# Turning normalized rows on VectorE and through DRAM instead of on TensorE

## The chip, the core and the metric

The kernel runs on one core of a Trainium2 chip. The time is device microseconds of one execution, the median of three runs. A profile is taken of a further execution; its rows are what this document reads. Engines are named as in the profile: PE is TensorE (PEld its weight loads), DVE VectorE, ACT ScalarE, POOL GpSimd, SP the engine that issues most DMAs; "SPq" is SP's queue.

## The reference

Four batches of 2048 tokens with 256 channels go through four residual steps. LN is a layer norm without learned scale, all in float32:

```
x = x + attention_a(LN(x))     # 16 heads of 16, causal softmax, q k v o projections
x = x + ffn(LN(x))             # sigmoid(W_r xr) * (W_v relu(W_k xk)^2), xr and xk mix x with the row before
x = x + attention_b(LN(x))     # keys: decayed sum, length 1, per-head scale; queries are the next keys;
                               # values: mixed with the next row, length 1, per-head scale
x = x + ffn(LN(x))
```

## The kernel before

**The main loop.** The two attentions of four batches are eight; each is worked in four groups of four heads, which makes NI x NHG = 32 "instances". An instance has NG = 68 groups, in four chunks of queries (qc), whose last slots are 4, 17, 38 and 67. In each slot TensorE computes the scores of the group three ahead (AHEAD = 3, three pairs of PSUM banks) and the probability-value products of its own; ScalarE does the exponentials (L828); GpSimd masks the diagonal groups (L731), which are groups 0 to 4, 13 to 17, 34 to 38 and 63 to 67; VectorE takes a finished chunk out of PSUM with a transpose (`take`, L1493), normalizes it, and in odd instances turns it and hands it to SP, which stores it in `o_chan` (L494) two slots later.

**Side work.** Everything else is a `Job` of one chunk of 512 tokens of one batch, laid into the same slots:
- P: layer norm, turn to channel-major (`xT`), q, k and v projections of attention a (parts u0 to u3, v0, v1), a bound on the scores (n).
- MA: output projection of attention a (o0, o1), layer norm, turn into `xf`, the FFN (k0, k1, r0, r1, f0, f1), a second layer norm (lnb), a second turn into `xT`, keys and values of attention b (bk, bv, vt), their lengths, and the split of keys into three bfloat16 parts.
- MB: output projection of attention b and the second FFN.

Each job has a first slot t0 and a table of offsets (`T_P`, `T_P0`, `T_P1`, `T_M`, `T_B`, `T_END`). MA jobs and most MB jobs start 4 slots before an instance does, so offset 20 is slot 16. Every engine has a program of its own in order of slots (`interleaved`: the main loop's work of a slot first, then the jobs'). No engine counts slots at run time: each works through its own order as fast as its semaphore waits allow, so a wait holds all that stands behind it on that engine.

**Banks.** Six PSUM banks hold scores at any time; side parts use the one of banks 6 and 7 that the current chunk's products don't use. `free_bank` therefore makes a part wait for the take of the chunk before (`s_o`):

```
            def free_bank(part):
                if part.before:
                    pe.wait_ge(s_side[part.bank], part.before)
                if part.seg > 0:
                    pe.wait_ge(s_o, part.seg)
```

**Turns.** A turn is two parts of four TensorE transposes with an identity (`turn`, L884), each copied out of PSUM (`copy_out`, L1204, on VectorE; L771 on ScalarE for batch 0). There are 64: 16 in P jobs, 32 in MA jobs, 16 in MB jobs. In FFN jobs the difference with the row before follows (`buf_a`, L681 on GpSimd and L1329 on VectorE), then four products with mu (L1335), which k0 and r0 wait for.

**Lengths.** In an MA job GpSimd squares keys and values; VectorE reduces both (L1386, L1389), runs one Newton chain over 128 columns (`rsqrt`, L1171 to L1180, L1395 to L1401), gives GpSimd `v_fac` (which it waits for at "vb" to write `v_st`, L709), and scales the keys (L1413).

## Time and profile before

| | |
|---|---|
| median of 3 runs | 3010.7 us (3007.7 to 3011.1) |
| the profiled execution | 3010.8 us, span 3009.1 us |
| mean granted TensorE clock | 0.976 |
| busy: PE, PEld | 2862.4 us, 1302.0 us |
| busy: ACT, DVE, POOL | 2232.7, 1472.8, 817.1 us |
| DMA packets | 229828, 225 MB; SP's queue takes 25.3% of the 16 DMA engines' span |

A busy time is the union of an engine's instructions; matmuls overlap, so a busy TensorE needn't be at its peak. Idle time stands with the instruction that came after it, put down to the semaphore that ended it. In the groups of instructions "out<-in" names tiles, then partitions x elements. Instance n begins where ScalarE does its group 68 n.

### The profile page before, as it was taken

To read this page: it belongs to the slowest core of one execution; us is meant where nothing else is said; L and a number is where in the kernel's file an instruction comes from. 1 tells how busy PE (TensorE), PEld (TensorE's weight loads), DVE (VectorE), ACT (ScalarE), POOL (GpSimd) and SP (SyncE) were. 2 spreads that over 40 slices of the span, in tenths; PEclk is the share of its full clock that TensorE was granted. 3 is DMA by queue.
4 is the path that set the end of the run, shared out by engine and by line. 5 is a ranking of instruction groups with operands and counts; after the bars stand their busy time and mean duration, and the time that the engine had idled before them with its cause. 6 is when DMAs were issued, how large, how long until landed. Compare 5 with 4: busy or idle time off the path is not lost.

```text
span 3009.1 us, 99722 instructions
## 1 busy us (share of the span) xinstructions
PE 2862.4 (95%) x42984; PEld 1302.0 (43%) x42984; DVE 1472.8 (49%) x3579; ACT 2232.7 (74%) x2487; POOL 817.1 (27%) x1246
## 2 busy tenths in 40 slices
PE   6999999999999899998999999999999989999897
PEld 3444444444444344444444444444444434444343
DVE  5322346565556654445344434555665656523544
ACT  2799978787787478784788878778787856788472
POOL 4222223332323222221222222232333322322111
PEclk9999999999999899998999999999999999999898
DMA  5322312222222123222322223222222221222111
GB/s 136 106 83 81 95 53 78 70 73 67 81 71 60 52 67 103 81 76 67 95 81 74 82 89 94 64 78 68 63 75 71 73 66 52 72 72 85 41 62 41
DMA packets 229828, 225.34 MB, mean 75 GB/s; under 512 B 33221, under 2 KB 212933, under 8 KB 229320
## 3 DMA queue, kind: packets, MB, share of 16 engines
q1 hardware_dynamic: 228504, 217.47, 25.3%
q8 instruction: 356, 5.83, 0.8%
q14 instruction: 152, 1.25, 0.1%
q10 hardware_dynamic: 816, 0.79, 0.1%
HBM read 146.80 MB, written 71.32 MB: 72 GB/s over the span
## 4 chain that ended last, share of the span: by engine, by line
PE 72%; DVE 16%; issue 6%; ACT 4%; POOL 1%; SPq 0%; DVEq 0%; DMA 0%; ACTq 0%
PE ps L872 46%; PE ps L1103 23%; ACT probs L828 4%; DVE pmax L1434 3%; PE ps L884 3%; DVE xn L1198 2%; DVE nw_y L1180 1%; DVE nw_u L1178 1%; DVE ln_st L1186 1%; DVE nw_u L1176 1%; DVE x_buf L1315 1%; DVE o_blk L1493 1%; DVE k_blk L1413 1%; DVE nw_v L1389 1%; POOL buf_k L703 0%
## 5 line engine op out<-in xcount | busy, mean ns | idle before, releaser
L828 ACT ACTIVATE probs<-ps 128x1024 f32<-128x1024 f32 x2176 | 2083.1, 1059 | 477.7 <-PE ps L872 474.5
L872 PE MATMUL ps<-q_st,k_st 99*32 99x512 bf16 (+3 forms) x20480 | 1237.4, 349 | 5.0 <-issue 2.4
L1103 PE MATMUL ps<-probs,v_st 128*17 128x512 f32 (+3 forms) x10240 | 1160.7, 532 | 22.4 <-POOL probs L731 13.1
L872 PEld LDWEIGHTS ps<-q_st,k_st 99*32 99x32 bf16 x20480 | 567.0, 96 | 775.7 <-issue 449.6
L731 POOL TENSOR_SCALAR_AFFINE_SELECT probs<-probs 128x256 f32<-128x256 f32 (+1 forms) x896 | 433.4, 501 | 1138.7 <-ACT probs L828 1120.1
L1103 PEld LDWEIGHTS ps<-probs,v_st 128*17 128x17 f32 x10240 | 291.9, 98 | 272.2 <-issue 59.1
L872 PE MATMUL ps<-xT,wT 128*32 128x512 f32 x2048 | 242.6, 594 | 0.0
L1493 DVE STREAM_TRANSPOSE o_blk<-ps 128x512 f32<-128x512 f32 x128 | 91.0, 711 | 269.2 <-PE ps L1103 268.9
L657 POOL TENSOR_TENSOR parts<-rest,parts 128x512 bf16<-128x512 f32 x96 | 120.9, 1260 | 316.7 <-DVE parts L1221 316.7
L1348 DVE SCALAR_TENSOR_TENSOR buf_v<-buf_v,ps 128x512 f32<-128x512 f32 x64 | 44.0, 687 | 272.9 <-PE ps L872 272.9
L1315 DVE TENSOR_TENSOR x_buf<-x_buf,ps 128x512 f32<-128x512 f32 x64 | 43.8, 684 | 217.6 <-PE ps L872 207.2
L872 PE MATMUL ps<-wT,o_in 128*32 128x256 f32 x2048 | 124.3, 380 | 14.5 <-issue 14.5
L872 PE MATMUL ps<-buf_k,wT 128*32 128x512 f32 x1024 | 124.7, 609 | 8.2 <-DVE buf_k L1335 8.0
L872 PEld LDWEIGHTS ps<-xT,wT 128*32 128x32 f32 x2048 | 65.1, 109 | 139.8 <-issue 136.1
L872 PE MATMUL ps<-wT,buf_u 128*32 128x256 f32 x2048 | 121.9, 379 | 1.6 <-issue 1.6
L872 PE MATMUL ps<-wT,buf_a 128*32 128x256 f32 x2048 | 121.6, 379 | 0.6 <-issue 0.5
L884 PE MATMUL ps<-ident,xn 128*128 128x128 f32 x512 | 85.8, 293 | 34.7 <-DVE xn L1198 24.5
L792 ACT ACTIVATE buf_u<-ps 128x512 f32<-128x512 f32 x64 | 38.2, 597 | 99.9 <-PE ps L872 99.9
L884 PEld LDWEIGHTS ps<-ident,xn 128*128 128x128 f32 x512 | 55.8, 145 | 125.1 <-DVE xn L1198 63.1
L1216 DVE TENSOR_TENSOR rest<-ps,parts 128x512 f32<-128x512 f32 x64 | 44.1, 690 | 133.5 <-ACT parts L778 133.5
L681 POOL TENSOR_TENSOR buf_a<-xf 128x512 f32<-128x512 f32 x32 | 33.2, 1037 | 270.3 <-DVE xf L1204 255.5
L1198 DVE TENSOR_SCALAR xn<-x_buf,ln_mv,nw_y 128x256 f32<-128x256 f32 x256 | 99.3, 450 | 2.3
(140 smaller groups left out, 2148.9 us busy)
## 6 DMA issues: line engine op xcount, KB each, us to landing
part_a<-parts SPq DMA_DIRECT2D x192, 128.0 KB
x_buf<-in_L_attn_a_X SPq DMA_DIRECT2D x32, 512.0 KB, 4.6
q_st<-part_a SPq DMA_DIRECT2D x128, 128.0 KB
o_chan<-o_out SPq DMA_DIRECT2D x64, 256.0 KB, 2.4
o_in<-o_chan SPq DMA_DIRECT2D x64, 256.0 KB, 4.6
q_st<-part_b SPq DMA_DIRECT2D x128, 128.0 KB
k_st<-part_a SPq DMA_DIRECT2D x64, 192.0 KB, 2.9
part_b<-parts SPq DMA_DIRECT2D x96, 128.0 KB
```

The costliest lines, as they stand in the source:

```text
L657: pool.tensor_tensor(parts[:, u % NPARTS, 2, :], rest[:, u % 2, :], parts[:, u % NPARTS, 1, :], ALU.subtract).then_inc(s_low, 1)
L731: last = pool.affine_select(out=o, in_=o, compare_op=ALU.is_ge, fill=0.0, base=0, pattern=[[0, o.shape[1]], [1, P]], channel_multiplier=-1)
L828: nc.scalar.activation(probs[:, g % NP_BUF, :], ps[:, bk:bk + 2, :].rearrange("p a n -> p (a n)"), ACT.Exp, scale=SCALE[ATT[g // (NHG * NG ...
L872: last = pe.matmul(o[c:c + 32], kt[:, c:c + 32], q, **how)
L884: last = pe.transpose(ps[:, part.bank, tb * P:(tb + 1) * P], src[:, tb, kt * P:(kt + 1) * P], ident[:, :])
L1103: last = pe.matmul(ps[32 * j:32 * j + VW, bank, q0:q0 + w], v_st[:, k % 2, kb, hg * HG + j, :], p, start=(kb == 0), stop=(kb >= TB * qc), ...
L1198: last = nc.vector.tensor_scalar(xn[:, tb, :], x[:, tb, :], ln_mv[:, tb, 0:1], nw_y[:, tb:tb + 1], ALU.subtract, ALU.mult)
L1216: nc.vector.tensor_tensor(left, src, high, ALU.subtract).then_inc(s_side[part.bank], 1)
L1315: nc.vector.tensor_tensor(half(x, i), half(x, i), ps[:, part.bank, :], ALU.add).then_inc(s_side[part.bank], 1)
L1348: nc.vector.scalar_tensor_tensor(half(gate, i), half(gate, i), 1.0, ps[:, part.bank, :], ALU.add, ALU.mult).then_inc(s_side[part.bank], 1)
L1434: nc.vector.tensor_reduce(pmax[:, 1 if b0 else 0, qb:qb + 1], src, AX_X, ALU.max).then_inc(s_mx["used"], 1)
L1493: nc.vector.transpose(o_blk[:, sg % 2, :], ps[:, 6 + sg % 2, :]).then_inc(s_o, 1)
```

## The change

- 55 of the 64 turns go another way: VectorE transposes the normalized rows in 32x32 blocks inside SBUF (two instructions of 128x512, into `xt`, which is the buffer of `o_in`); SP stores them with four DMAs to a scratch tensor `norm_chan` in DRAM, each DMA one quarter of the partitions in pieces of 32 floats, so that DRAM holds them channel-major; SP waits for the stores and loads the 256x512 matrix back into `xT` or `xf` with one DMA. TensorE keeps the turns of P jobs of batch 0 and of the five jobs of table `T_END`.
- u0 and bk0 on TensorE, and the difference on VectorE and GpSimd, wait for that load (`turned`) instead of for a copy out of PSUM. `load_o` also waits for the last store from `xt`.
- The tables have new entries "tr" and "td" (SP's stores and load), and leave 16 slots or more from the layer norm to the first use.
- The lengths of keys and of values are two chains of 64 columns, at offset 61 ("klen", which scales the keys at once) and 78 ("vlen"); "vb" moves from 70 to 80.

```
-T_P = {"load": -10, "ln": 0, "t0": 8, "t1": 12, "u0": 14, "u1": 16, "u2": 18, "u3": 20, "v0": 22, "v1": 24, "n": 28,
-       "flag": 31, "store": 4}
+T_P = {"load": -10, "ln": 1, "tr": 7, "td": 11, "u0": 17, "u1": 19, "u2": 21, "u3": 23, "v0": 25, "v1": 27, "n": 30,
+       "flag": 33, "store": 4}
-T_P1 = {"load": -10, "ln": 0, "t0": 8, "t1": 10, "u0": 13, "u1": 18, ...
+T_P1 = {"load": -10, "ln": 0, "tr": 6, "td": 10, "u0": 20, "u1": 22, ...
-T_M = {"load": -10, "o0": 0, "o1": 2, "ln": 3, "t0": 12, "t1": 14, "diff": 13, "shift": 16, "k0": 18, "k1": 20, "r0": 26,
-       "r1": 28, "f0": 30, "f1": 32, "out": 34}
-T_B = {"lnb": 32, "bt0": 40, "bt1": 46, "bk0": 48, "bk1": 50, "bv0": 52, "bv1": 54, "w": 55, "u": 57, "vt0": 59, "vt1": 61,
-       "len": 63, "keys": 69, "split": 91, "vb": 70, "low": 94, "store": 98}
+T_M = {"load": -10, "o0": 0, "o1": 2, "ln": 3, "tr": 10, "td": 14, "diff": 20, "shift": 20, "k0": 23, "k1": 25, "r0": 27,
+       "r1": 29, "f0": 31, "f1": 33, "out": 35}
+T_B = {"lnb": 33, "btr": 41, "btd": 45, "bk0": 51, "bk1": 53, "bv0": 55, "bv1": 57, "w": 58, "u": 60, "vt0": 63, "vt1": 65,
+       "klen": 61, "vlen": 78, "split": 91, "vb": 80, "low": 94, "store": 98}
...
+            def store_turn(n):
+                sp.wait_ge(s_xt, n + 1)
+                if n >= 2:
+                    sp.wait_ge(*turned(n - 2))
+                for i in range(4):
+                    dst = xt_d[n % 2].rearrange("(j c) (t i e) -> i c t j e", c=32, t=TB, i=4)[i]
+                    src = xt[32 * i:32 * (i + 1), :].rearrange("c (t j e) -> c t j e", t=TB, e=32)
+                    sp.dma_start(dst, src).then_inc(s_xt_out[n % 2], 16)
+
+            def load_turn(n, dst):
+                sp.wait_ge(*stored_turn(n))
+                sp.dma_start(dst, xt_d[n % 2].rearrange("(k p) n -> p k n", p=P)).then_inc(s_turned[n % 2], 16)
...
+            def turn_blocks(j, name):
+                n = j.at[name + "_turn"]
+                dve.wait_ge(s_ln, j.at[name] + 1)
+                if n >= 1:
+                    dve.wait_ge(*stored_turn(n - 1))
+                rows = xn[:, :, :].rearrange("p t d -> p (t d)")
+                for h in range(2):
+                    last = nc.vector.transpose(xt[:, h * CH:(h + 1) * CH], rows[:, h * CH:(h + 1) * CH])
+                last.then_inc(s_xt, 1)
...
 (VectorE, m_job)
                 normalize(j)
-                for kt in range(KT):
-                    yield j.t0 + j.off[f"t{kt}"]
-                    copy_out(j.at[f"t{kt}"], xf[:, kt, 1:CH + 1])
+                if "tr" in j.off:
+                    turn_blocks(j, "ln")
+                    yield j.t0 + j.off["diff"]
...
-                dve.wait_ge(*emptied(j.at["t1"]))
+                dve.wait_ge(*(turned(j.at["ln_turn"]) if "tr" in j.off else emptied(j.at["t1"])))
                 step(nc.vector.tensor_tensor(buf_a[:, 1, :], xf[:, 1, 1:CH + 1], xf[:, 1, 0:CH], ALU.subtract))
                 yield j.t0 + j.off["shift"]
...
-                yield j.t0 + j.off["len"]
+                yield j.t0 + j.off["klen"]
                 nh = TB * H
                 dve.wait_ge(s_ksq, 2 * (j.at["ma"] + 1))
+                of_keys, of_values = slice(0, nh), slice(nh, 2 * nh)
+                inverse_lengths(buf_a, of_keys)
...
+                yield j.t0 + j.off["vlen"]
                 dve.wait_ge(s_vsq, 2 * (j.at["ma"] + 1))
+                inverse_lengths(buf_k, of_values)
```

`inverse_lengths(sq, at)` is the old chain (reduce, floor, `rsqrt`, product, epsilon, reciprocal) on the columns `at`.

## Rows read from the trace of the kernel before

**Rows 1.** The page: busy time of each engine, its share, instructions.

```profile
PE 2862.4 (95%) x42984; PEld 1302.0 (43%) x42984; DVE 1472.8 (49%) x3579; ACT 2232.7 (74%) x2487; POOL 817.1 (27%) x1246
```

**Rows 2.** The chain that ended last, shares of the span by line.

```profile
by line: PE ps L872 46.0%; PE ps L1103 23.0%; issue 6.1%; ACT probs L828 3.7%; DVE pmax L1434 2.6%; PE ps L884 2.5%; DVE xn L1198 1.7%; DVE nw_y L1180 1.2%; DVE nw_u L1178 1.2%; DVE ln_st L1186 1.2%; DVE nw_u L1176 1.1%; DVE x_buf L1315 0.8
```

**Rows 3.** The waits: total us, times, longest.

```profile
ACT probs L828 <- PE ps L872: 474.5, 484, 33.0
...
PE ps L884 <- DVE xn L1198: 24.5, 19, 9.5
DVE k_blk L1413 <- issue: 22.1, 7, 3.3
...
PE ps L884 <- DVE o_blk L1493: 10.1, 14, 1.2
```

**Rows 4.** Groups of instructions by line and shape: busy, mean ns, idle before.

```profile
L731 POOL TENSOR_SCALAR_AFFINE_SELECT probs<-probs 128x256 f32<-128x256 f32 x768 | 353.9, 478 | 1126.5 <-ACT probs L828 1117.5
...
L884 PE MATMUL ps<-ident,xn 128*128 128x128 f32 x512 | 85.8, 293 | 34.7 <-DVE xn L1198 24.5 <-DVE o_blk L1493 10.1
...
L681 POOL TENSOR_TENSOR buf_a<-xf 128x512 f32<-128x512 f32 x32 | 33.2, 1037 | 270.3 <-DVE xf L1204 255.5 <-PE ps L884 14.8
```

**Rows 5.** Timeline of ScalarE in instances 1, 5 and 13: start, us, what.

```profile
206.30 34.03 ACT L828 ACTIVATE probs<-ps 128x1024 f32<-128x1024 f32 x37 [0.20 <-PE ps L872]
...
475.65 9.47 ACT L828 ACTIVATE probs<-ps 128x1024 f32<-128x1024 f32 x10 [2.88 <-PE ps L872]
...
1209.38 9.27 ACT L828 ACTIVATE probs<-ps 128x1024 f32<-128x1024 f32 x10 [1.52 <-PE ps L872]
1218.97 1.94 ACT L828 ACTIVATE probs<-ps 128x1024 f32<-128x1024 f32 x2 [0.31 <-PE ps L872]
1221.39 3.77 ACT L828 ACTIVATE probs<-ps 128x1024 f32<-128x1024 f32 x4 [0.49 <-PE ps L872]
```

**Rows 6.** Timeline of VectorE in instance 13.

```profile
1215.18 1.38 DVE L1198 TENSOR_SCALAR xn<-x_buf,ln_mv,nw_y 128x256 f32<-128x256 f32 x4
1216.47 0.71 DVE L1493 STREAM_TRANSPOSE o_blk<-ps 128x512 f32<-128x512 f32 x1
...
1218.17 0.71 DVE L1507 STREAM_TRANSPOSE o_out<-o_norm 128x512 f32<-128x512 f32 x1
...
1222.46 1.63 DVE L1335 SCALAR_TENSOR_TENSOR buf_k<-buf_a,mu,xf 128x512 f32<-128x512 f32 x2
```

**Rows 7.** DMA issues: count, KB each, median us to landing.

```profile
x_buf<-in_L_attn_a_X SPq DMA_DIRECT2D x32, 512.0 KB, 4.6
...
x_mid<-x_buf SPq DMA_DIRECT2D x16, 512.0 KB, 2.9
...
probs<-in_L_attn_b_W_v SPq DMA_DIRECT2D x1, 256.0 KB, 8.2
```

**Rows 8.** Timeline of SP's queue, 0 to 60 us.

```profile
53.46 1.83 SPq L449 DMA_DIRECT2D part_a<-parts  x3
```

**Rows 9.** DMA from 12 to 13 us, the 64-byte pieces of a weight.

```profile
DMA packets 1810, 0.10 MB, mean 97 GB/s; under 512 B 1805, under 2 KB 1810, under 8 KB 1810
```

**Rows 10.** Timeline of VectorE at the end of instance 13's FFN.

```profile
1246.46 0.69 DVE L1348 SCALAR_TENSOR_TENSOR buf_v<-buf_v,ps 128x512 f32<-128x512 f32 x1 [2.04 <-PE ps L872]
...
1252.46 2.15 DVE L1198 TENSOR_SCALAR xn<-x_buf,ln_mv,nw_y 128x256 f32<-128x256 f32 x4
```

**Rows 11.** Timeline of VectorE, the lengths of an MA job.

```profile
550.47 1.22 DVE L1389 TENSOR_REDUCE nw_v<-buf_k 128x64 f32<-128x1024 f32 x1 [4.78 <-POOL buf_k L703]
...
558.20 0.37 DVE L1401 TENSOR_TENSOR v_fac<-nw_y,v_scale 128x64 f32<-128x64 f32 x1
```

**Rows 12.** Timeline of GpSimd, the scaled values of that kind of job.

```profile
472.49 1.94 POOL L709 TENSOR_TENSOR v_st<-buf_v,v_fac 128x1024 f32<-128x1024 f32 x1 [0.16 <-DVE v_fac L1401]
```

**Rows 13.** TensorE's timeline; then a stretch: busy PE, PEld, DVE, ACT, POOL; clock, DMA.

```profile
741.09 1.05 PE L1103 MATMUL ps<-probs,v_st 128*17 128x512 f32 x8 [2.64 <-DVE x_buf L1315]
...
742.00:746.00 4.00, 4.00 (x48) 2.10 (x44) 3.55 (x18) 1.94 (x2) 0.00 (x0) 0.57 0.22 72
```

More of the change, by code:

```diff
@@ L267, in hybrid_kernel @@
         o_d = nc.dram_tensor("o_chan", (2, KT, P, S), F32, kind="Internal").ap()
+        xt_d = nc.dram_tensor("norm_chan", (2, D, CH), F32, kind="Internal").ap()
         x2_d = nc.dram_tensor("x_mid", (B, S, D), F32, kind="Internal").ap()
@@ L350, in hybrid_kernel @@
         s_ln = sem("norm_ready")
+        s_xt = sem("norm_blocks_turned")
+        s_xt_out = [sem(f"norm_blocks_stored{i}") for i in range(2)]
+        s_turned = [sem(f"norm_turned{i}") for i in range(2)]
         s_part = sem("part_in_psum")
@@ L438, in x_stores, with load_channels @@
                 return sum(1 for j in JOBS[n % 2:n + 1:2] if j.kind != "P")
+            def store_turn(n):
[9 more added lines that the diff above has]
+                sp.dma_start(dst, xt_d[n % 2].rearrange("(k p) n -> p k n", p=P)).then_inc(s_turned[n % 2], 16)
+            def load_channels(j, n):
+                users = [i for i in JOBS if i.kind != "MB" and i.at["chan"] == j.at["chan"] - 2]
+                for i in users:
+                    sp.wait_ge(s_part, i.at["v1" if i.kind == "P" else "bv1"].n + 1)
+                load_turn(n, xT[:, j.at["chan"] % 2, :, :])
             def p_job(j):
@@ L479, in load_o @@
                     sp.wait_ge(s_part, FFN[f - 1].at["o1"].n + 1)
+                before = [i.at[name + "_turn"] for slot, at, name in LN_ORDER for i in [JOBS[at]]
+                          if slot < j.t0 + j.off["load"] and name + "_turn" in i.at]
+                if before:
+                    sp.wait_ge(*stored_turn(before[-1]))
                 k = ATT.index(("A" if j.kind == "MA" else "B", j.b))
@@ L910, in p_job @@
                     if at == j.off[f"u{i}"]:
-                        for kt in range(KT):
-                            pe.wait_ge(*emptied(j.at[f"t{kt}"]))
+                        if "tr" in j.off:
+                            pe.wait_ge(*turned(j.at["ln_turn"]))
+                        else:
+                            for kt in range(KT):
+                                pe.wait_ge(*emptied(j.at[f"t{kt}"]))
                         if j is JOBS[0]:
@@ L962, in m_job @@
                 src = xT[:, j.at["chan"] % 2]
-                for kt in range(KT):
-                    if at == j.off[f"bt{kt}"]:
-                        pe.wait_ge(s_ln, j.at["lnb"] + 1)
-                        turn(j.at[f"bt{kt}"], xn, kt)
                 for w, name in ((BK, "bk"), (BV, "bv")):
@@ L969, in m_job @@
                         if at == j.off[f"{name}{m}"]:
-                            for kt in range(KT):
-                                pe.wait_ge(*emptied(j.at[f"bt{kt}"]))
+                            pe.wait_ge(*turned(j.at["lnb_turn"]))
                             project_channels(j.at[f"{name}{m}"], w, m, src)
@@ L1358, in m_job @@
                 normalize(j)
-                for kt in range(KT):
-                    yield j.t0 + j.off[f"bt{kt}"]
-                    copy_out(j.at[f"bt{kt}"], xT[:, j.at["chan"] % 2, kt, :])
+                turn_blocks(j, "lnb")
                 for m in range(KT):
```

95 lines of the change are left out of this document (58 added, 37 removed).

## The prediction

> **What bounds the kernel now.** I read the page first, then the chain, the waits, the costs by group, and the timelines of one piece of work. TensorE is busy 95% of the span, ScalarE 74%, VectorE 49%, GpSimd 27% [rows 1]; the chain that ended last runs 71% through TensorE's matmuls, and the turns (L884) hold 2.5% of it [rows 2]; ScalarE waits 474.5 us for TensorE [rows 3]. To be seen there: nothing but TensorE's own order of work counts, and what another engine does counts only where TensorE waits for it.
>
> One number orders the rest. Where no side work is due, ScalarE's activations follow each other every 0.904 us (37 of them in 34.03 us, the last one lasting 1.03) [rows 5]; I call that one slot. Each side part put into TensorE's stream adds its time to that, and a wait of TensorE adds directly, since ScalarE holds only three groups ahead. 68 slots are an instance, 32 instances the kernel.
>
> **What the change takes away.**
> (a) 55 of the 64 turns leave TensorE (12 P jobs, 27 M jobs, 16 second turns of MA jobs). In instance 13, which begins at 1205.92, ten activations up to the first half of the turn take 1218.97 - 1209.38 = 9.59 us against 10 x 0.904 = 9.04, the next two 1221.39 - 1218.97 = 2.42 against 1.81 [rows 5]: 0.55 + 0.61 = 1.16 us. Times 55: 64 us. Two other rows bound it: L884's busy time of 85.8 us, 440/512 of it 74 us [rows 4], and its waits for xn and o_blk, 34.6 us together, of which a single one is 9.5 [rows 3]. I keep 64.
> (b) The one chain of lengths now ends inside the next job's o0 and o1. ScalarE's wait there is 2.88 us in instance 5, which follows an MA job, and 1.52 in instance 13, which doesn't [rows 5]; with the keys' chain at offset 61 the 1.36 us go, 16 times: 22 us.
> (c) VectorE's keys product waits 22.1 us in 7 places for nothing that the profile shows [rows 3], and in one such place TensorE waited 2.64 us behind it [rows 13]. That product is moved away: 7 x 2.64 = 19 us.
> Together 105 us. VectorE itself gains nothing: 110 copies out of PSUM become as many transposes of 0.71 us [rows 6], and a second Newton chain comes on top, which lies beside other work until it is asked for below.
>
> **What it adds: the round trip.** After xn, VectorE turns blocks (2 x 0.71 = 1.4 us). Then SP issues four stores of 1024 pieces of 128 bytes, waits for them, and issues the load of 512 KB. Nothing before shows such a store. An issue takes 0.6 us (three in 1.83) [rows 8], so the last one starts 1.8 us after the first. 64-byte pieces went through at 1810 packets in 1 us [rows 9], so 4096 need 2.3 us: no more than the issuing. A 512 KB store in large pieces lands after 2.9 us [rows 7]; with 0.6 for the short pieces the store costs 1.8 + 2.9 + 0.6 = 5.3 us. The load is that of x_buf, 4.6 us [rows 7]. I take 9.9 us. Bounds: 1.8 + 2.9 + 2.9 = 7.6, every DMA at the price of the cheapest 512 KB; and 8.2 + 8.2 = 16.4, both at the price of the slowest load of weights, which lay in a full queue [rows 7]. The value is near the low end since these DMAs find the 16 engines a quarter busy (25.3%, the table), not full.
>
> The Trainium skill (DMA: Bandwidth & Descriptors, Specifications) asks for at least 512 bytes a piece and says that smaller ones are read, modified and written. No row here shows a slow short write. By that rule the store would be dearer than its packets, and it is a rival below.
>
> **Where the round trip ends, in the M jobs.** I lay the new tables on instance 13. xn is written at 1216.56 [rows 6], the blocks are turned at 1218.0. In even instances SP stores from 1218.1, and the turned rows are there at 1228.0. In odd ones SP's store of o stands ahead of it (slot 6, same slot, earlier in the order), and waits for the head outputs that VectorE now takes after the blocks: 2.4 us (1216.47 to 1218.88) [rows 6] and 0.35 of issue, so 1230.7. Behind VectorE's new wait stand, in this order, the difference (1.04 us on GpSimd beside it [rows 4]), four shift products of 0.82 us [rows 6] with a small copy, and the take of slot 17 with its transpose of 0.71: 5.4 us, so 1233.4 or 1236.1. k0 needs that take: its bank is that of the segment before, and free_bank waits for s_o. TensorE is there much sooner: group 19 starts at 1209.38 + 17 x 0.904 = 1224.8, ends 1.0 later, and slot 19's own work is 0.9: 1226.7. The stall is 6.7 us in even instances, 9.4 in odd ones. 11 M jobs are of this kind (6 even, 5 odd): 87 us.
>
> **The 16 M jobs after an MA job** have one thing more. "vlen" stands in slot 6, behind the take of slot 4 (VectorE free at 1219.6 or 1220.4). The old chain took from 550.47 to 558.57, 8.1 us, on 128 columns [rows 11]; on 64 I estimate 6.3, since a narrow instruction keeps its fixed part. GpSimd's vb in slot 8 waits for it (1225.9 or 1226.7) and lasts 1.94 [rows 12]. Queued behind vb are the masks of groups 13 to 17, 0.48 us an instruction [rows 4]; TensorE needs the second in slot 14, where it arrives at about 1221.7, and gets it at 1228.8 or 1229.6. The five mask instructions that are left, then the difference, then the 4.4 us of VectorE give k0 at 1236.5 or 1237.3: 10.2 us late on average, whatever the DMAs take below about 10 us. Times 16: 163 us.
>
> **The second turn and the P jobs.** From the last projection's end T (1246.4, where VectorE takes it up) to xn written is 8.2 us (1252.46 + 2.15) [rows 10]; in MA jobs half the statistics are done earlier, so I take 7.5. No queue is in the way here: SP's loads of slot 36 are free long before. P of batches 2 and 3: T + 8.2 + 1.5 + 9.9 = T + 19.6 against u0 17 slots later, T + 15.4: 4.2 us, 8 times, 34 us. MA: T + 18.9 against bk0 18 slots later, T + 16.3: 2.6 us, 16 times, 42 us. P of batch 1 has its rows only just in time, and about 2 us late in two odd instances: 4 us.
>
> Sum of stalls: 87 + 163 + 42 + 34 + 4 = 330 us.
>
> **The clock.** In the place of [rows 13] TensorE had waited 2.64 us; in the four microseconds after it the granted clock was 0.57, the level of 1.2 GHz for most of them, so some 1.7 us of its work were lost. The 27 long stalls are each longer than that one: 27 x 1.7 = 46 us, with nothing for the short ones.
>
> The Trainium skill (TensorE: Matmul & The Clock Gate, Part 1) says that the throttled state is the default and activity releases it. The trace agrees (0.57 behind the wait) [rows 13]; by it, a kernel with more waits also loses clock.
>
> **Total.** 330 + 46 - 105 = +271 us. The profiled execution took 3010.8 us (span 3009.1), practically the median of 3010.7: 3280 us.
>
> **Rivals.**
> 1. The short writes are slow. If a 128-byte piece costs the store like the queue of weights (8.2 us for the store, and 8.2 for a load behind it), every round trip is 6.5 us longer; the first turn then loses some 13 us in an even M job and 16 in an odd one, the second turns 9 and the P jobs 6 to 11, about 650 us in all: 3600. Half of that excess gives 3440. For it: nothing in the trace prices such a write. Against it: the 1810 packets a microsecond. Chance of more than 3360: 0.18.
> 2. The round trip is short, 7.6 us. The M jobs after MA keep their 163 us, since GpSimd and VectorE are late there without DMA; the other M jobs lose 4.4 and 7.1 us (62), P 1.9 (15), the second turn 0.3 (5), and the clock may hold: 245 - 105 = +140, 3150 us. Chance of 3020 to 3190: 0.16.
> 3. Faster: SP, VectorE and GpSimd reach their waits early enough that nothing new reaches TensorE. Then only the 105 us count, 2906 us. It decides in one place: the turned rows would have to be there 5.4 us before slot 19's work is done, at 1221.3, that is 3.3 us after the blocks are turned; one 512 KB load alone takes 4.6 [rows 7]. It also needs vb's wait away. Against it is the order of VectorE's program. Chance 0.08.
> 4. Gains and stalls cancel (3005 to 3017): 0.02.
> The forecast with its own spread, 3190 to 3360: 0.56. The range 3120 to 3480 leaves out the faster cases, the lowest part of the short round trip and the upper end of rival 1. 0.2%, or 6 us, is what a measurement can tell. Faster 0.08, same 0.02, slower 0.90.
>
> **What would show it.** L884 falls from 512 to 72 matmuls. New waits: TensorE's k0 (L872) for o_blk of VectorE, 7 to 10 us; L1103 for GpSimd's masks by some 7 us in instances 5 to 12 and 21 to 28; u0 and bk0 for xT, 2 to 4 us; VectorE for the DMA into xf. Instances 0 to 3 should change by less than 2 us each, instances 16 to 19 grow by about 10. The granted clock falls from 0.976 to about 0.95. I am wrong if the load of norm_chan lands within 5 us of the blocks being turned, if the vb wait doesn't hold the masks, or if a store of short pieces lands far later than 5.3 us after its first issue.

## Result, and the profile after

The changed kernel takes 3307.1 us (median; 3304.3 to 3307.7) against 3010.5 (3007.7 to 3011.1) for the kernel before in the same session: ratio 1.0984, 95% interval 1.0967 to 1.1002. It is 297 us slower. The forecast was 3280 us and slower. The profiled execution spans 3305.2 us, 296.1 more than before.

Lines of the changed kernel: the activations are L880, side matmuls and scores L924, TensorE's turns L936, products with values L1153, masks L783, block transposes L1272, the take L1555, the difference L1404 (VectorE) and L733 (GpSimd), the products with mu L1410, vb L761, SP's stores L462 and load L466.

The page of the changed kernel: busy time of each engine (compare [rows 1]), the packets, and the chain that ended last by engine. The line of that chain for the kernel before stands last.

```profile
PE 2901.6 (88%) x42544; PEld 1266.6 (38%) x42544; DVE 1517.5 (46%) x3819; ACT 2213.7 (67%) x2487; POOL 796.1 (24%) x1246
DMA packets 473589, 283.00 MB, mean 86 GB/s; under 512 B 262901, under 2 KB 442613, under 8 KB 473080
...
PE 55%; DVE 23%; DMA 10%; issue 5%; SPq 3%; POOL 2%; ACT 1%; DVEq 0%; POOLq 0%; ACTq 0%
...
PE 72%; DVE 16%; issue 6%; ACT 4%; POOL 1%; SPq 0%; DVEq 0%; DMA 0%; ACTq 0%
```

Its waits: engine and line, what it waited for, us in all, times, longest (compare [rows 3]).

```profile
ACT probs L880 <- PE ps L924: 598.5, 326, 30.7
...
PE ps L1153 <- POOL probs L783: 112.3, 40, 7.3
PE ps L924 <- DMA xT<-norm_chan: 96.3, 27, 5.9
PE ps L924 <- DVE o_blk L1555: 91.5, 18, 10.3
...
DVE x_buf L1386 <- issue: 38.9, 11, 3.9
```

TensorE was 95% busy and is now 88%; its mean granted clock was 0.976 and is now 0.928. The chain that ended last went through TensorE for 72% of the span and through VectorE for 16%; now it is 55%, 23%, and 10% through DMAs. Three new waits of TensorE hold 300.1 us: masks, the turned rows in `xT`, and the take that k0's bank needs. Only the first had a counterpart before, 13.1 us.

The timeline of instance 13, which follows no MA job: SP's queue, then VectorE, then TensorE.

```profile
1305.59 3.85 SPq L462 DMA_DIRECT2D norm_chan<-o_in  x4
1312.01 0.39 SPq L466 DMA_DIRECT2D xf<-norm_chan  x1
...
1301.49 1.30 DVE L1272 STREAM_TRANSPOSE o_in<-xn 128x512 f32<-128x512 f32 x2
...
1316.41 0.69 DVE L1404 TENSOR_TENSOR buf_a<-xf 128x512 f32<-128x512 f32 x1 [11.31 <-DMA xf<-norm_chan]
1318.03 1.42 DVE L1410 SCALAR_TENSOR_TENSOR buf_k<-buf_a,mu,xf 128x512 f32<-128x512 f32 x2 [0.93 <-POOL buf_a L733]
...
1320.88 0.71 DVE L1555 STREAM_TRANSPOSE o_blk<-ps 128x512 f32<-128x512 f32 x1
...
1321.73 3.64 PE L924 MATMUL ps<-buf_k,wT 128*32 128x512 f32 x16 [9.08 <-DVE o_blk L1555]
```

The instance begins at 1290.80. The blocks are turned 12.0 us later, the stores are issued at 14.8 (SP waited for the store of o), the difference starts at 25.6 and k0 at 30.9; the forecast had 12.1, 24.8 for the rows and 30.2. TensorE's wait is 9.08 us where 9.4 was forecast. The clock in that place, four microseconds a row; columns as in [rows 13].

```profile
1314.00:1318.00 4.00, 0.00 (x0) 0.00 (x0) 0.69 (x1) 0.00 (x0) 1.54 (x1) 0.79 0.70 187
1318.00:1322.00 4.00, 0.27 (x4) 0.23 (x8) 3.87 (x8) 0.00 (x0) 0.00 (x0) 0.50 0.00 0
1322.00:1326.00 4.00, 4.00 (x25) 1.06 (x21) 1.22 (x3) 0.57 (x1) 0.00 (x0) 0.50 0.24 79
1326.00:1330.00 4.00, 4.00 (x52) 1.59 (x48) 0.00 (x0) 2.44 (x4) 1.04 (x1) 0.93 0.39 124
```

The granted clock falls to 0.50, the level of 1.2 GHz, within the wait, and holds it for over four microseconds of full work behind it: 16 matmuls of k0 take 3.64 us instead of 1.9.

Instance 5, which follows an MA job (it begins at 487.14), GpSimd and TensorE:

```profile
506.98 1.93 POOL L761 TENSOR_TENSOR v_st<-buf_v,v_fac 128x1024 f32<-128x1024 f32 x1 [12.81 <-DVE v_fac L1473]
508.97 0.31 POOL L765 MEMSET v_st<- 1x272 f32 x1
509.25 2.78 POOL L783 TENSOR_SCALAR_AFFINE_SELECT probs<-probs 128x256 f32<-128x256 f32 x7
...
510.06 1.91 PE L1153 MATMUL ps<-probs,v_st 128*17 128x512 f32 x8 [6.72 <-POOL probs L783]
...
517.94 1.92 PE L924 MATMUL ps<-buf_k,wT 128*32 128x512 f32 x16 [0.49 <-DVE o_blk L1555]
```

GpSimd waits for the values' factors, runs vb, then hands out the masks; TensorE waits 6.72 us for them and only 0.49 more at k0. These are the two places that the forecast named, though it had put 3.1 us at the second. Over all 16 such instances the masks' wait is 5.2 to 7.3 us, 102.2 in all, and k0's 3.2 in all.

### The profile page after: what moved, and what is told of

It is laid out like the page before. It is cut to its first block, busy times and chain, and to the rows that moved or that the text cites. A ratio compares the mean times of both kernels' runs of the same rounds, so it can differ in the third digit from the quotient of the medians.

```text
span 3305.2 us, 99271 instructions
## 1 busy us (share of the span) xinstructions
PE 2901.6 (88%) x42544; PEld 1266.6 (38%) x42544; DVE 1517.5 (46%) x3819; ACT 2213.7 (67%) x2487; POOL 796.1 (24%) x1246
## 4 chain that ended last, share of the span: by engine, by line
PE 55%; DVE 23%; DMA 10%; issue 5%; SPq 3%; POOL 2%; ACT 1%; DVEq 0%; POOLq 0%; ACTq 0%
PE ps L924 38%; PE ps L1153 15%; DMA norm_chan<-o_in 4%; DMA xT<-norm_chan 3%; SPq L462 3%; DVE pmax L1496 2%; DVE xn L1261 2%; DVE o_in L1272 2%; DMA xf<-norm_chan 2%; DVE ln_st L1249 2%; DVE nw_y L1230 1%; DVE o_blk L1555 1%; DVE nw_u L1226 1%; DVE nw_u L1228 1%; ACT probs L880 1%
## 5 line engine op out<-in xcount | busy, mean ns | idle before, releaser
L880 ACT ACTIVATE probs<-ps 128x1024 f32<-128x1024 f32 x2176 | 2062.1, 1085 | 600.4 <-PE ps L924 598.5
L1153 PE MATMUL ps<-probs,v_st 128*17 128x512 f32 (+3 forms) x10240 | 1183.5, 541 | 119.0 <-POOL probs L783 112.3
L924 PE MATMUL ps<-q_st,k_st 99*32 99x512 bf16 (+3 forms) x20480 | 1243.2, 355 | 8.8 <-issue 8.5
L924 PEld LDWEIGHTS ps<-q_st,k_st 99*32 99x32 bf16 x20480 | 572.4, 98 | 821.9 <-issue 432.3
L783 POOL TENSOR_SCALAR_AFFINE_SELECT probs<-probs 128x256 f32<-128x256 f32 (+1 forms) x896 | 399.0, 464 | 1099.7 <-ACT probs L880 1093.5
L1153 PEld LDWEIGHTS ps<-probs,v_st 128*17 128x17 f32 x10240 | 290.3, 100 | 398.9 <-POOL probs L783 152.1
L924 PE MATMUL ps<-xT,wT 128*32 128x512 f32 x2048 | 276.7, 668 | 96.3 <-DMA xT<-norm_chan 96.3
L924 PE MATMUL ps<-buf_k,wT 128*32 128x512 f32 x1024 | 144.2, 688 | 99.9 <-DVE o_blk L1555 91.5
L924 PEld LDWEIGHTS ps<-xT,wT 128*32 128x32 f32 x2048 | 64.5, 116 | 240.3 <-issue 120.2
L1555 DVE STREAM_TRANSPOSE o_blk<-ps 128x512 f32<-128x512 f32 x128 | 88.8, 693 | 125.4 <-PE ps L1153 125.1
L1289 DVE TENSOR_TENSOR rest<-ps,parts 128x512 f32<-128x512 f32 x64 | 44.2, 690 | 213.8 <-ACT parts L830 213.8
L924 PE MATMUL ps<-wT,o_in 128*32 128x256 f32 x2048 | 126.0, 385 | 0.3 <-issue 0.3
L924 PE MATMUL ps<-wT,buf_u 128*32 128x256 f32 x2048 | 122.6, 379 | 1.6 <-issue 1.6
L924 PE MATMUL ps<-wT,buf_a 128*32 128x256 f32 x2048 | 122.4, 379 | 0.6 <-issue 0.5
L830 ACT CAST parts<-ps 128x512 bf16<-128x512 f32 x64 | 37.5, 586 | 120.6 <-PE ps L924 120.6
L745 POOL TENSOR_TENSOR buf_a<-k_blk 128x512 f32<-128x512 f32 x32 | 33.3, 1040 | 326.5 <-DVE k_blk L1445 326.5
L737 POOL TENSOR_TENSOR buf_u<-buf_u 128x512 f32<-128x512 f32 x64 | 73.7, 1151 | 154.4 <-ACT buf_u L844 154.4
L924 PEld LDWEIGHTS ps<-buf_k,wT 128*32 128x32 f32 x1024 | 35.8, 120 | 190.4 <-issue 180.8
```

Of the source, the lines that this page charges most:

```text
L737: pool.tensor_tensor(buf_u[:, m, :], buf_u[:, m, :], buf_u[:, m, :], ALU.mult).then_inc(s_kact, 1)
L783: last = pool.affine_select(out=o, in_=o, compare_op=ALU.is_ge, fill=0.0, base=0, pattern=[[0, o.shape[1]], [1, P]], channel_multiplier=-1)
L880: nc.scalar.activation(probs[:, g % NP_BUF, :], ps[:, bk:bk + 2, :].rearrange("p a n -> p (a n)"), ACT.Exp, scale=SCALE[ATT[g // (NHG * NG ...
L924: last = pe.matmul(o[c:c + 32], kt[:, c:c + 32], q, **how)
L1153: last = pe.matmul(ps[32 * j:32 * j + VW, bank, q0:q0 + w], v_st[:, k % 2, kb, hg * HG + j, :], p, start=(kb == 0), stop=(kb >= TB * qc), ...
L1555: nc.vector.transpose(o_blk[:, sg % 2, :], ps[:, 6 + sg % 2, :]).then_inc(s_o, 1)
```

## Experiments

All ratios are to the kernel before on the same chip.

| run | us | ratio, 95% interval | clock |
|---|---|---|---|
| no_dram | 3064.0 | 1.0178, 1.0161 to 1.0195 | 0.955 |
| no_dram_vb | 3050.1 | 1.0137, 1.0120 to 1.0154 | 0.962 |
| vb_late | 3355.0 | 1.1150, 1.1132 to 1.1169 | 0.927 |
| take_first | 3339.4 | 1.1098, 1.1079 to 1.1116 | 0.928 |
| lengths_only | 3092.9 | 1.0278, 1.0262 to 1.0294 | 0.962 |
| lengths_early | 2995.3 | 0.9952, 0.9938 to 0.9965 | 0.977 |
| lengths_mid | 2987.5 | 0.9928, 0.9914 to 0.9941 | 0.976 |
| hybrid | 2995.5 | 0.9954, 0.9940 to 0.9967 | 0.977 |
| warm | 3235.7 | 1.0741, 1.0722 to 1.0759 | 0.956 |
| mb_slack | 3172.2 | 1.0534, 1.0516 to 1.0553 | 0.946 |
| after_early | 3407.9 | 1.1327, 1.1310 to 1.1344 | 0.921 |
| after_mid | 3400.9 | 1.1294, 1.1277 to 1.1311 | 0.919 |

**no_dram: the changed kernel without its DMAs.**

```
-  xt[:, half] <- transpose(rows[:, half]);  SP: 4 stores to norm_chan, 1 load into xf or xT
+  xf[:, half, 1:] or xT[..][:, half] <- transpose(rows[:, half]);  turned(n) = VectorE's own count
```

> The kernel after the change with the round trip through DRAM left out: VectorE writes its 32x32 blocks straight into xT or xf, no store and no load of norm_chan, everything else (tables, chains of lengths) as changed. The turned rows then hold blocks in the wrong places, so the output isn't the reference's. Theory (the round trip and what stands behind its wait cost most): the 11 first turns without an MA job before them, the P jobs and the second turns stop waiting; what is left of the loss is GpSimd's vb in front of the masks, 16 times some 8.5 us. 3010.5 - 105 + 136 = about 3040 us. Rival (the loss is in the new tables and VectorE's longer program, not in the DMAs): over 3200 us. L1272 still runs, so VectorE's work is unchanged.

Beside the code shown, a wait of `load_o` for the stores is left out. It takes 3064.0: 243 of the 297 us go with the DMAs. It is 24 us above the theory, and the rival (over 3200) falls. What is left of the waits is, in that kernel's waits of TensorE:

```profile
PE ps L1139 <- POOL probs L769: 119.6, 39, 7.7
...
PE ps L910 <- DVE o_blk L1546: 19.7, 11, 1.8
```

TensorE waits as long for the masks as it does with the DMAs (112.3). So the vb chain is a cause of its own, enough for that wait by itself.

**vb_late: the changed kernel with vb behind the masks.**

```
-       "klen": 61, "vlen": 78, "split": 91, "vb": 80, ...
+       "klen": 61, "vlen": 78, "split": 91, "vb": 90, ...
```

> The kernel after the change with vb at offset 90 (slot 18 of the next instance, behind the masks of groups 13 to 17) instead of 80. Theory (the two waits lie one behind the other, and the first only hides the second): the 7 to 9 us before group 18 go in the 16 instances after an MA job, and k0's wait there grows from under 1 us to the 9 to 12 us that it has in the other jobs: 3307 us, within 15 either way. Rival (vb costs its own 8 us each time): 3307 - 16 x 8.5 = 3170 us.

3355.0, 48 us worse than the changed kernel and beyond both theories. The masks' wait is gone (12.6 us), and k0's wait went from 91.5 to 241.1 us, 27 times: the round trip is enough by itself too. The time of vb doesn't vanish either: it now runs beside VectorE's products with mu, of which those that write `buf_k` take 1160 ns on average instead of 749:

```profile
L1410 DVE SCALAR_TENSOR_TENSOR buf_k<-buf_a,mu,xf 128x512 f32<-128x512 f32 x64 | 71.7, 1160 | 25.6 <-POOL buf_a L733 25.0
```

**take_first: the changed kernel with difference and products behind the take of slot 17.**

```
-T_M = {..., "diff": 20, "shift": 20, "k0": 23, ...
+T_M = {..., "diff": 22, "shift": 22, "k0": 23, ...
```

> The kernel after the change with diff and shift of T_M at offset 22 instead of 20, so that VectorE takes the chunk of slot 17 before it waits for the turned rows. Theory (k0 waits for the take only because it is queued behind VectorE's wait): k0's wait changes from o_blk to buf_k and ends with the second shift product, 2.3 us earlier (a second pair of products, the copy and the transpose less): 11 x 2.3 + 16 x 0.6 and a little clock, about -40 us, 3267 us. Rival (the round trip itself is all): no change, 3307 us.

3339.4, 32 us worse, where 40 better was forecast. The 11 jobs that follow no MA job did gain, 1.0 to 3.1 us each in groups 22 to 45. The 16 others lost 1.8 to 4.8 there, and VectorE's timeline in instance 5 shows how:

```profile
512.54 0.72 DVE L1555 STREAM_TRANSPOSE o_blk<-ps 128x512 f32<-128x512 f32 x1 [9.11 <-PE ps L1153]
```

There the chunk's last products wait for masks behind vb, so the take that now stands in front waits for them, 9.11 us, with the turned rows already there (GpSimd took up its difference at 508.9); difference and products come behind it. The new order is right for one kind of job and wrong for the other.

**no_dram_vb: both at once, no DMAs and vb late.**

```
-  "vb": 80   (in the kernel of no_dram)
+  "vb": 90
```

> Both of no_dram and vb_late together: blocks written straight to xT and xf (output not the reference's), vb at offset 90. Theory: nothing new reaches TensorE, and only the 105 us of gains are left: about 2910 us, with k0 to be seen without a wait. Rival (the stalls have a third source, such as the tables): over 2950 us.

3050.1: the theory (2910) falls, the rival stands. A third delay is left, in the jobs after an MA job. VectorE, then GpSimd, in instance 5:

```profile
489.92 3.06 DVE L1401 SCALAR_TENSOR_TENSOR buf_k<-buf_a,mu,xf 128x512 f32<-128x512 f32 x2 [0.93 <-POOL buf_a L719]
...
494.42 0.71 DVE L1546 STREAM_TRANSPOSE o_blk<-ps 128x512 f32<-128x512 f32 x1
...
488.63 1.26 POOL L719 TENSOR_TENSOR buf_a<-xf 128x512 f32<-128x512 f32 x1 [1.91 <-DVE v_fac L1464]
489.85 1.93 POOL L747 TENSOR_TENSOR v_st<-buf_v,v_fac 128x1024 f32<-128x1024 f32 x1
```

GpSimd's difference waits for the values' factors, since those squares share its buffer; then vb lies beside VectorE's two products, which take 3.06 us instead of 1.41; the take that k0 needs comes last. TensorE still waits 109.7 us for o_blk, 90.0 of them in the 16 jobs after an MA job. By this timeline it is the offset of vlen that does it, not vb's alone. No run moved vlen in this kernel; the next three move it where the turns are TensorE's.

**lengths_only: the kernel before with the change's lengths and no other part.**

```
-       "len": 63, "keys": 69, "split": 91, "vb": 70, ...
+       "klen": 61, "vlen": 78, "split": 91, "vb": 80, ...
```

> The kernel before with the second part of the change alone: two chains of lengths at the changed kernel's offsets (klen 61, vlen 78, vb 80); every turn stays on TensorE and no table moves. Theory, that the values' chain at offset 78 is what holds GpSimd's masks in the 16 jobs after an MA job, whatever the turns do: in each of them VectorE's values chain (5.5 us) ends about 5 us after it is due, vb takes 1.9 us more, the second mask of group 13 and the copies of the turn are late, 7 to 9 us a job, against the gains (b) and (c), 41 us together: 3090 to 3150. Rival A, the changed kernel's masks are late only because its tables push the values' chain behind the block transposes: here VectorE begins it in time and only the gains are left, 2970. Rival B: the waits come but overlap the old waits for xn, 3010 to 3050. In the profile the theory wants PV (L1103) waiting for GpSimd's masks, and only in instances 5 to 12 and 21 to 28.

3092.9, 83.6 us above the kernel before: just within the theory's range, but not at its place. The masks wait only 7.5 us in all. TensorE's timeline in an instance after an MA job, and its waits:

```profile
488.22 1.09 PE L884 MATMUL ps<-ident,xn 128*128 128x128 f32 x4 [4.84 <-issue]
...
PE ps L884 <- issue: 75.4, 16, 5.3
```

The second half of TensorE's turn waits for VectorE to copy the first (at 487.43), which stood behind the values' chain (481.98 to 487.52). The profile names no releaser for that wait; that it is the copy is read from the two timelines. A values' chain at 78 holds TensorE with TensorE's turns (here) and with blocks that need no DMA (no_dram). In the changed kernel itself, moving it gives nothing (after_mid, below).

**lengths_early: the same split, placed early.**

```
+       "klen": 58, "vlen": 63, "keys": 85, "split": 91, "vb": 70, ...
```

> The kernel before with the lengths in two chains placed early: keys at offset 58, values at 63, vb stays at 70, the keys product is a part of its own at 85, and the key factors lie in columns that the values' chain doesn't write. Every turn stays on TensorE. Theory: only the gains (b) 22 us and (c) 19 us of the prediction come, 2965 to 2985. Rival: the chains take up the slots in which VectorE writes the second turn's and the values' copies, which TensorE waits for, so the 41 us are spent again: 3000 to 3020. In the profile the theory wants ScalarE's wait at the start of instance 5 down by about 1.4 us and no idle time without a releaser ahead of the keys product.

2995.3, faster than the kernel before, but 14 us of the 41. The wait at the start of an instance fell by 0.5 us instead of 1.4, in 12 of the 16: the values' chain ended at 645.2 in instance 7, and the copy of o0, for which o1 waits, stood right behind it. The keys product at 85, ahead of the take of slot 17, cost 0.7 us in 13 of the 16 jobs.

**lengths_mid: keys' chain ahead of the mixing of values.**

```
+       "klen": 56, "keys": 60, "vlen": 63, "split": 91, "vb": 70, ...
```

> The kernel before with two chains of lengths once more, all turns on TensorE, vb at 70: the keys' chain at 56, ahead of the mixing of values, in VectorE's idle time there (3.7 and 2.7 us in the trace of the last such kernel), the keys product at 60, the values' chain at 63. In the earlier version the keys' chain began at 631.5 only, behind that mixing, and the values' chain ended at 645.0, 0.1 us ahead of the copy of o0 that TensorE's o1 waits for (16 times some 1 us, and 3 us later for the keys product). Theory: with the keys' chain out of the way the values' chain is bound by its squares (637.5 in that instance) and ends near 643, before o0 is done, so gains (b), 17 us as the changed kernel shows it, and (c), 15 us, both come: 2970 to 2985. Rival: the chain in front of the mixing makes TensorE's turns of values late, and it is at 2995 or above.

2987.5: 2.5 us above the expected span, 8 below lengths_early, the fastest of all. ScalarE's second wait in instance 5 is down from 2.88 us to that of a job after none, while the mixing, now behind the keys' chain, makes TensorE's turn of values late by 0.8 to 0.9 us in 14 of the 16 jobs (against the kernel before, groups 45 to 68 take 13.8 us more in all, groups 0 to 14 take 35.0 less).

```profile
473.61 7.44 ACT L828 ACTIVATE probs<-ps 128x1024 f32<-128x1024 f32 x8 [1.52 <-PE ps L872]
```

**after_early and after_mid: the changed kernel with its lengths placed early, in two ways.**

```
after_early  "klen": 60, "vlen": 67, "keys": 86, "split": 91, "vb": 74, ...
after_mid    "klen": 59, "keys": 63, "vlen": 67, "split": 91, "vb": 74, ...   (keys' chain ahead of the mixing)
```

> The changed kernel with its lengths placed early: keys' chain at 60, values' at 67, vb at 74, keys product a part of its own at 86; the turns go through DRAM as before. So in the 16 jobs after an MA job neither the values' chain nor vb stands in the slots of the first turn. Prediction's reading (the 10.2 us of those jobs are vb's, whatever the DMAs take): they fall to the 6.7 or 9.4 us of the other jobs, 16 x 2.1 = 34 us less, 3270. Theory after the runs so far: the mask waits (about 7 us) go but the same time comes back at k0, where the round trip ends 8 to 9 us late, and what vb held the queue for is worth only some 1 to 3 us a job: 3260 to 3300, with k0 waiting for o_blk 27 times by about 9 us and no wait for masks above 1 us. Rival: the early chains collide with the second turn and the values' parts, as a new wait of TensorE at bk0 or vt0: above 3310.

> The changed kernel with the lengths placed so that they stand in nobody's way: keys' chain at 59, ahead of the mixing of values, keys product at 63, values' chain at 67, vb at 74. The turns go through DRAM. It repeats the run with early lengths (3408) without its flaw, o1's wait of 4.1 us behind the values' chain in 16 jobs (46.8 us in groups 0 to 14 with its clock). Theory: 3350 to 3370, that is, nothing is won against 3307: with the masks in time k0 waits for the round trip itself, as in the jobs that follow no MA job, so vb's wait lay wholly under the round trip. Rival, the prediction's own reading (vb's wait is worth 10.2 us a job, whatever the DMAs take, the round trip 6.7 or 9.4): at or below 3290.

3407.9 and 3400.9, 101 and 94 us worse than the changed kernel: my expectation was missed twice, by 108 and by 31 us (the first rival had the sign, but named bk0 and vt0 for the collision, where it is o1). One part of it was right. The waits of TensorE in after_mid:

```profile
PE ps L924 <- DVE o_blk L1556: 240.0, 27, 11.7
PE ps L924 <- DMA xT<-norm_chan: 99.9, 27, 6.0
...
PE ps L1153 <- POOL probs L783: 10.4, 32, 1.7
```

With the masks in time k0 waits for the round trip in all 27 jobs, by 8.9 us on average, more than the 5.2 to 7.3 us that the masks had taken. The rest is two collisions. The values' chain can't end before its squares (697.6, 3 us before instance 7 begins) allow, and o0's copy stands behind it at 703.66; o1 waits 2.44 us and takes 3.61 us instead of 1.9, and up to 4.4 us are lost in an instance (1.7 of them are the lower clock behind the wait). And vb moved beside the layer norm, the chain that the round trip starts from. GpSimd, VectorE twice, TensorE:

```profile
712.06 1.93 POOL L761 TENSOR_TENSOR v_st<-buf_v,v_fac 128x1024 f32<-128x1024 f32 x1
...
712.15 1.87 DVE L1221 TENSOR_SCALAR nw_y<-nw_v 128x4 int32<-128x4 int32 x1
714.05 0.17 DVE L1223 TENSOR_SCALAR nw_y<-nw_y 128x4 int32<-128x4 int32 x1
...
704.44 3.61 PE L924 MATMUL ps<-wT,o_in 128*32 128x256 f32 x32 [2.44 <-issue]
```

An instruction of 128x4 lasts 0.17 us when GpSimd is idle. The one that begins 0.09 us after vb lasts 1.87 and ends as vb ends (714.02 and 713.99).

**warm: the changed kernel with idle matmuls in TensorE's waits.**

```
+  for _ in range(count):    # 7 before k0 (11 jobs), 5 before u0 (batches 2, 3), 3 before bk0
+      pe.matmul(ps[:, bank of the next scores, :], ident, wT, start=True, stop=True)
```

> The changed kernel with idle matmuls (identity by weights, 128x512 in float32, into the bank of the next scores, which overwrite it) put in front of the new waits of TensorE: 7 before k0 in the 11 M jobs that don't follow an MA job, 5 before u0 in P jobs of batches 2 and 3, 3 before bk0. The computation is unchanged. The time at half clock is 333 us longer after the change, and about 214 us of matmuls more run in it. Theory, that the clock's loss is an own term of the result (about 107 us in all): where the matmuls fill a wait the clock stays at its upper level and the work behind it is done at full speed, 3 to 4 us a long wait and 1 to 2 a short one: 3220 to 3260, mean clock near 0.96. Rival: the low clock only coincides with waits that hold the time anyway (VectorE and GpSimd are late by the same amount whatever TensorE's speed): 3300 to 3315, the clock up all the same. Second rival: the fillers are longer than the waits and the time rises above 3320.

3235.7, 71 us less, as the theory had it. Its four executions lie far apart (3226.9 to 3249.8); the profiled one, which the rows below are from, is the slowest of them and 57 us shorter than the changed kernel's. TensorE in instance 13 (the idle matmuls first), and the clock there:

```profile
1309.74 6.28 PE L947 MATMUL ps<-wT,ident 128*128 128x512 f32 x14
1317.75 1.92 PE L928 MATMUL ps<-buf_k,wT 128*32 128x512 f32 x16 [1.73 <-DVE o_blk L1572]
```

```profile
1314.00:1318.00 4.00, 2.27 (x9) 0.76 (x11) 3.85 (x8) 0.00 (x0) 0.01 (x1) 1.00 0.00 0
1318.00:1322.00 4.00, 4.00 (x48) 1.66 (x44) 1.24 (x3) 2.27 (x3) 1.04 (x1) 1.00 0.38 101
```

The clock stays at 1.00 and k0 takes 1.92 us, not 3.64. Summed over the trace, the time at the lower level is 287.7 us here, 478.8 in the changed kernel and 146.0 before. In the places of the 11 long waits it fell from 99.0 to 10.2 us. The theory's shares come out otherwise: the long waits gave back 1.6 us each (3 to 4 expected), and groups 45 to 68, where the short ones lie, 49.3 us. The mask waits in the 16 jobs after MA jobs were left as they were.

**mb_slack: the changed kernel with ten more slots in the 11 MB jobs.**

```
+T_MB = {**T_M, "diff": 30, "shift": 30, "k0": 33, "k1": 35, "r0": 37, "r1": 39, "f0": 41, "f1": 43, "out": 45}
```

> The changed kernel with a table of its own for the 11 MB jobs that start with an instance: difference and shift at 30, k0 at 33, the rest 10 slots later too. MA and P jobs as in the changed kernel. Theory: k0's wait in the 9 such jobs that don't follow an MA job goes with the slack, and its clock with it: the gap before k0's slot is 13.9 us in odd instances and 10.8 in even ones, where 2.5 are its own work, so 5 x 11.4 + 4 x 8.3 = 90 us less, 3217; 3200 to 3240. Rival: the wait moves on with the work (the take of slot 17 or P's parts come late instead), above 3280.

3172.2, 135 us less; 90 were expected. Its waits of TensorE:

```profile
PE ps L925 <- DMA xT<-norm_chan: 70.0, 19, 5.5
PE ps L925 <- DVE o_blk L1556: 16.0, 4, 8.8
```

k0's wait is down to 16.0 us in 4 places (91.5 in 18), 14.8 of them in the two MA jobs whose table wasn't changed, and groups 22 to 45 are 75.8 us shorter (22 to 26 by 122.9, while 26 to 45, where the work has moved to, are 47.1 longer). The 54 us I hadn't expected lie in groups 45 to 68 of the 8 instances with P jobs of batches 2 and 3: the wait for `xT` came 27 times and comes 19 times. P's table is the same; what changed is VectorE's order. P's layer norm used to stand behind the FFN's last part (in the changed kernel's instance 12: x_buf at 1240.85, statistics at 1241.46, blocks at 1248.33). Now it stands ahead of the FFN's last two parts and starts as soon as the products with mu are done, here in instance 13:

```profile
1325.30 1.41 DVE L1250 BATCH_NORM_STATS2 ln_st<-x_buf 128x6 f32<-128x256 f32 x4
...
1331.05 1.30 DVE L1273 STREAM_TRANSPOSE o_in<-xn 128x512 f32<-128x512 f32 x2
...
1341.61 0.69 DVE L1424 SCALAR_TENSOR_TENSOR buf_v<-buf_v,ps 128x512 f32<-128x512 f32 x1 [9.26 <-PE ps L925]
```

P's load is issued at 1345.83 and u0 begins at 1355.51 without a wait. An engine's place in the order decides when a round trip starts, not the slot in the table.

**hybrid: lengths_mid, and the DRAM turn in those 11 MB jobs alone, with that slack.**

```
+T_MB = {**T_M, "tr": 10, "td": 14, "diff": 30, ..., "out": 45}      # as above; MA and P keep t0, t1 on TensorE
+del T_MB["t0"], T_MB["t1"]
```

> The kernel with the lengths of the run above, and the turn through DRAM in the 11 MB jobs alone that start with an instance, where nothing hangs on their end: their difference and shift stand at 30, k0 at 33 and all that follows 10 slots later than in the changed kernel, so that the turned rows have 19 slots, 17 us, after the stores' place in the tables instead of 9. All other turns are TensorE's. Theory, that the round trip costs only where its end is waited for: the 11 jobs lose TensorE's turn (27 jobs gave back 39.7 us in slots 10 to 14, 1.47 us a job) and get nothing for it: 16 us below the run above, 2955 to 2970. Rival: contention (its DMAs beside SP's other loads, two transposes of VectorE ahead of a take, GpSimd's parts now ahead of the masks of slots 34 to 38) takes it back: equal to the run above or slower.

2995.5, 8 us slower than lengths_mid: the rival. The TensorE turn's time does come back (1.1 us a job in groups 0 to 14), and nothing waits for the round trip. But the FFN's parts cost more where they are now. With P jobs, P's turn at slot 37 falls beside f0: that gap is 4.1 us, 1.0 more than both by themselves. Without them, in instance 29, f1 lies so near the end of the chunk that the next chunk's products begin at 2692.85, 0.10 us after VectorE was done with f1's bank (2692.10, 0.65 us); the profile names no releaser for that wait of 1.03 us. Instances 28 and 29 come out as long as in lengths_mid, within 0.1 us, and instance 13, with a P job, 0.8 longer. Instances 12, 14, 16 and 30 are 1.4 to 2.7 us longer; why, stays open.

## Why the prediction was right, and where it wasn't

The total was forecast as +271 us and is +297. The waits are the ones that the prediction named, in the places that it named. That the sum is so close is partly luck: the stalls were put 43 us too high and the clock some 61 too low. (A small slip beside it: 37 activations in 34.03 us, the last of 1.03, make 0.917 us each. The spacing that most of them have is the 0.904 that the prediction goes on with.)

1. **Turns off TensorE (a).** Forecast 64 us, 1.16 a job. ScalarE's activations in slots 10 to 14 of the 27 M jobs, above 0.904 us each, held 39.7 us before and nothing after: 1.47 a job (the hybrid shows 1.1). TensorE's turns are busy 13.2 us instead of 85.8 [rows 4]. That is a quarter above the forecast. For 24 of the other turns no run stands alone; in no_dram, groups 36 to 68 of those 27 instances are 38.4 us shorter than before, 1.6 a turn.
2. **Start of an instance (b).** Forecast 22 us; the first two gaps of the 16 instances fell from 47.8 to 30.9 us above the slot: 17.
3. **VectorE's wait for nothing (c).** Forecast 19 us. The stretch behind it (groups 2 to 8 of the 16 instances, above the slot) fell from 21.4 to 6.4 us, 15; but its cause was misread. The wait wasn't that of the keys product: after the change it stands ahead of x_buf, 11 times, 38.9 us, where before the keys product [rows 3] and x_buf had 10 and 32.0 together:

```profile
DVE x_buf L1315 <- issue: 9.9, 3, 3.8
```

   In the program that place is the branch of the row maxima, once an instance, which the profile doesn't count as work. The trace holds the branch too: in instance 6 of the kernel before, the comparison (L1469) ends at 559.75, and the next instruction of VectorE, of any kind, stands at 562.79, the first behind the jump (L1482). Of the 32 such branches 28 jump over the block: 14 of them were followed by 2.6 to 3.5 us of nothing and 14 by 0.5. No run removed the branch. What the move gained is the work that stood behind the wait.
4. **The round trip.** Forecast 9.9 us. From the first store's issue to the load's issue the median is 5.55 us (forecast 5.3), and the load lands after 4.2 to 4.3 (forecast 4.6), 9.8 in all:

```profile
norm_chan<-o_in SPq DMA_DIRECT2D x220, 128.0 KB, 2.9
xT<-norm_chan SPq DMA_DIRECT2D x28, 512.0 KB, 4.2
xf<-norm_chan SPq DMA_DIRECT2D x27, 512.0 KB, 4.3
```

   Rival 1, a store of 8.2 us, falls: 225,280 pieces of 128 bytes went out, and a store of 128 KB landed 2.9 us after its issue. But that is a quarter of the bytes for which [rows 7] show 2.9 us, and the short pieces do move more slowly. A microsecond of instance 13 in which only they moved, then one of the load behind them, in pieces of 1 and 2 KB (the last two columns are the share of the DMA engines and GB/s):

```profile
1310.00:1311.00 1.00, 1.00 (x28) 0.50 (x20) 0.00 (x0) 1.00 (x2) 0.00 (x0) 1.00 0.95 156
1314.00:1315.00 1.00, 0.00 (x0) 0.00 (x0) 0.00 (x0) 0.00 (x0) 0.00 (x0) 1.00 0.99 376
```

   Nearly all engines are busy in both, at 156 GB/s and at 376. At 156 GB/s the 512 KB of four stores take 3.4 us (an estimate), hardly more than SP takes to issue them (2.8 to 4.4 us, median 2.95), so little of it shows. The Trainium skill (DMA: Bandwidth & Descriptors, Specifications) puts the smallest transfer for line rate at 512 bytes. The trace agrees as far as the rate goes. Rival 2, a trip of 7.6 us, falls too.
5. **11 M jobs after none.** Forecast 87 us; k0's waits in these jobs are 88.2 (7.0 on average in even instances, 9.2 in odd ones). Right, and no_dram and mb_slack show the cause.
6. **16 M jobs after an MA job.** Forecast 10.2 us each, 163 in all: 7.1 at the masks and 3.1 more at k0. The masks take 6.4 on average and k0 adds 0.2, 105 us in all, so this term was 58 us too large. The masks are near: seven go through in 2.78 us, 0.40 each where I had 0.48, and the chain took 5.5 us (501.36 to 506.90) where I had 6.3. What failed is the 3.1 us at k0. In instance 5 k0 began 30.8 us after the instance's start, as forecast (30.6 to 31.4), but TensorE came there at 30.3 and not at 27.9. It reaches that place 1.0 us later than forecast in any job (21.85 us after the start in instance 13, where I had 20.8), and the work between the masks and k0 began at the lower clock. So part of the clock's loss lies under k0's wait and was counted twice. That vb alone is enough is shown (no_dram); what I hadn't said is that the DMAs alone are enough too (vb_late, after_mid). The two waits lie over each other: to take vb's away gives nothing.
7. **Second turns and P jobs.** Forecast 42 + 34 + 4 = 80 us; the wait for `xT` is 54.7 + 36.7 + 4.9 = 96.3.
8. **The clock.** Forecast 46 us, 1.7 for each of 27 long stalls and nothing for the short ones. This is the term that failed most. The time at the lower level grew by 332.8 us; TensorE was busy 326.6 us of it against 112.8 before. Of these 213.8 us more at half speed half is lost, 107 us by this estimate. Another count agrees: TensorE's busy time grew by 39.2 us although turns of 72.6 us had left it, 112 together. The trace tells where it lies. In groups 14 to 36 of the 27 instances TensorE has the same work before and after; it is idle there 195.8 us longer and busy 55.9 us longer, 2.1 for each long stall, not far from the 1.7. In groups 36 to 68 it is busy 53.3 us longer than in no_dram, 2.2 for each of the 24 waits for `xT` there, 3.8 us long on average. So the step that failed is the "nothing for the short ones". The warm run gave back 71 without touching the 16 mask waits.

Of the signs that the prediction gave, the granted clock fell to 0.928, not to about 0.95; instances 16 to 19 grew by 14.0 to 18.5 us, not by about 10, since the wait for `xT` and its clock come on top; and instance 3 grew by 4.9, not by less than 2.

The balance: stalls of 91.5 + 112.3 - 13.1 + 96.3 = 287 us, the clock's 107, and gains of 39.7 + 38.4 + 17 + 15 = 110, make 284, against 296 between the spans; 12 us stay unexplained. The forecast had 330, 46 and 105. Of the rivals, the faster case would have needed the rows 3.3 us after the blocks; with ten more slots the wait goes (mb_slack), and then what TensorE gets back is spent elsewhere (hybrid).

Open: what TensorE would gain without the branch, since no run took it away, why instances 12, 14, 16 and 30 of the hybrid are longer, and how much of the clock's loss the 16 mask waits hold, which the warm run left alone.

## What to carry to other kernels

Moving work off the bound engine is worth what it holds there, 1.1 to 1.6 us a turn here. A 9.8 us round trip in its place must end before anyone asks, counted in microseconds at that place and not in slots. Every engine that runs its program in order hands such a wait on to all that is queued behind it. When two waits lie over each other, test them together, and count a clock term for every wait of the bound engine, the short ones too. Of the change, the split of the lengths was the useful part: placed where VectorE is idle it is 0.7% faster than before, at the change's own offsets 2.8% slower.
